# A two-layer graph attention kernel: where the first norm's steps, the softmax reciprocals and the adjacency mask are made

## The reference

```python
h = relu(layernorm(x)); q, k, v = heads(h@Wq+bq), heads(h@Wk+bk), heads(h@Wv+bv)   # 16 heads of 32
scores = where(adj == 0, -inf, q @ k.T / sqrt(32))
x = x + (softmax(scores, -1) @ v) @ Wo + bo
h = relu(layernorm(x))
alpha = maximum((h@wq) @ (h@wk).T, 0) * (adj != 0)
alpha = softmax(alpha, axis=1)                       # over the rows
x = x + alpha @ (h @ weight)
```

## Time and profile before

| | |
|---|---|
| median of 3 runs | 1620.14 us (1619.84 to 1623.53) |
| profiled execution | 1615.62 us |
| its span, first to last instruction | 1613.8 us |
| TensorE (PE) busy | 1498.3 us, 93% |
| VectorE busy | 1316.8 us, 82% |
| ScalarE busy | 1129.5 us, 70% |
| GpSimd busy | 1018.6 us, 63% |
| granted TensorE clock, mean | 0.996 of full |
| HBM read and written | 57.94 and 16.78 MB, 46 GB/s |

### The profile page before, as it was taken

How to read it: one execution, slowest core, us unless ns; L and a number is a source line. 1 busy time by engine, 2 the same in 40 slices (tenths; PEclk the granted TensorE clock), 3 DMA queues, 4 the chain that set the end, 5 groups by cost and what they waited for, 6 DMA issues and landing times.

```text
span 1613.8 us, 50717 instructions
## 1 busy us (share of the span) xinstructions
PE 1498.3 (93%) x16561; PEld 1102.2 (68%) x16561; DVE 1316.8 (82%) x4202; ACT 1129.5 (70%) x2477; POOL 1018.6 (63%) x1286
## 2 busy tenths in 40 slices
PE   2889999999999999999999999999999999999996
PEld 1556777776777767677777677776667777767763
DVE  6788888888888888888888888888888888888773
ACT  3657776777777777777777777777777777777761
POOL 1556667667666766666766766676666676666561
PEclk9999999999999999999999999999999999999998
DMA  8758767666667765766766666676676676676660
GB/s 234 134 105 143 140 129 156 149 141 145 137 130 149 156 148 128 151 139 129 157 149 140 146 137 129 151 156 145 129 151 137 130 158 149 139 147 137 122 123 33
DMA packets 656197, 226.27 MB, mean 140 GB/s; under 512 B 611488, under 2 KB 627872, under 8 KB 656160
## 3 DMA queue, kind: packets, MB, share of 16 engines
q1 hardware_dynamic: 636848, 188.57, 58.1%
q10 hardware_dynamic: 19312, 37.23, 7.9%
HBM read 57.94 MB, written 16.78 MB: 46 GB/s over the span
## 4 chain that ended last, share of the span: by engine, by line
PE 53%; DVE 27%; issue 11%; ACT 4%; POOL 1%; DMA 1%; DVEq 1%; ACTq 0%; POOLq 0%; SPq 0%
PE ring L409 43%; DVE wk_raw L865 9%; PE pv L484 3%; PE score L465 3%; DVE heads_t_lo L959 2%; PE ring L519 2%; DVE newton L908 2%; DVE stage L946 2%; DVE o_sum L880 2%; DVE work L985 1%; DVE l_max L1000 1%; PE pv L486 1%; ACT val L668 1%; DVE e_lo L1016 1%; POOL wv_raw L1124 1%
## 5 line engine op out<-in xcount | busy, mean ns | idle before, releaser
L1124 POOL TENSOR_TENSOR wv_raw<-wk_raw,wv_raw 128x512 f16<-128x512 f32 x512 | 594.2, 1163 | 428.7 <-ACT wv_raw L639 428.5
L626 ACT ACTIVATE wk_raw<-wk_raw,least 128x256 f32<-128x256 f32 x1024 | 458.9, 497 | 8.4 <-DVE least L865 8.3
L865 DVE CUSTOM_DVE_ANT_0 wk_raw<-score,far,undo_score 128x256 f32<-128x256 f32 x1024 | 443.8, 477 | 11.7 <-DVE far L1036 11.4
L639 ACT ACTIVATE wv_raw<-wk_raw 128x512 f16<-128x512 f32 x512 | 320.4, 626 | 9.5 <-issue 4.5
L484 PE MATMUL pv<-val,turned 128*128 128x65 f16 x2048 | 185.8, 192 | 25.5 <-DVE o_sum L880 21.3
L484 PEld LDWEIGHTS pv<-val,turned 128*128 128x128 f16 x2048 | 148.3, 97 | 88.7 <-issue 39.6
L1143 POOL TENSOR_TENSOR heads_out<-o_sum,o_rcp 128x64 f32<-128x64 f32 x512 | 154.4, 323 | 76.2 <-DVE o_sum L880 72.7
L409 PE MATMUL ring<-wv_hi,h 128*128 128x256 f16 x1024 | 188.8, 273 | 1.6 <-DVE wv_lo L828 1.6
L409 PE MATMUL ring<-h,wq_hi 128*128 128x256 f16 x1024 | 175.5, 273 | 7.6 <-DVE wk_lo L828 7.6
L486 PE MATMUL pv<-val,turned 128*128 128x33 f16 x2048 | 177.9, 179 | 0.0
L409 PE MATMUL ring<-h,wk_hi 128*128 128x256 f16 x1024 | 175.1, 273 | 0.0
(11 more groups left out here) (147 smaller groups left out, 3570.9 us busy)
## 6 DMA issues: line engine op xcount, KB each, us to landing
xin<-x_dram ACTq DMA_DIRECT2D x32, 512.0 KB, 3.7
out_dram<-xo SPq DMA_DIRECT2D x32, 512.0 KB, 3.6
xa<-x_dram ACTq DMA_DIRECT2D x31, 512.0 KB, 4.1
adj_in<-adj_dram SPq DMA_DIRECT2D x32, 256.0 KB, 2.8
turned<-wv_raw SPq DMA_TRANSPOSE x512, 3.1
adjt_in<-adj_t_dram SPq DMA_DIRECT2D x32, 256.0 KB, 3.2
wq_raw<-wq_dram SPq DMA_DIRECT2D x2, 512.0 KB, 6.0
wk_raw<-wk_dram SPq DMA_DIRECT2D x2, 512.0 KB, 7.6
```

Source lines behind the costliest of these rows:

```text
L626: last = nc.scalar.activation(probs[:, at, q, :], probs[:, at, q, :], ACT.Exp, bias=least[:, at, q:q + 1], scale=-1.0)
L639: nc.scalar.activation(halves[:, at, :, 0, :], probs[:, at, :, :], ACT.Copy).then_inc(hi["p"], 1)
L865: last = nc.vector.tensor_tensor_reduce(out=probs[:, at, q, :], in0=score[u % GROUP][:, q * NODES:(q + 1) * NODES], in1=far[:, q, :], scal ...
L1124: nc.gpsimd.tensor_tensor(halves[:, at, :, 1, :], probs[:, at, :, :], halves[:, at, :, 0, :], ALU.subtract).then_inc(lo["p"], 1)
```

## The change

Four things:

- `far` is written by GpSimd itself, in step 11 in place of step 8, after the last mask of the present graph has been made (`masked`). `far_next` and VectorE's copy are gone; VectorE's first mask of the next graph waits for GpSimd (`far_ok`), and so does SyncE's load of the next `adj_in`.
- The Newton step of the first norm is taken by GpSimd at the head of `first_normalise`, as six instructions on two columns, the last four of which wait for the one before. Both are in step 12 now (`NORM1`), behind the writing of `far` in GpSimd's order. VectorE's `reciprocal_deviation` is left for the second norm only.
- `second_reciprocal` is put ahead of the mask in VectorE's step 12.
- The low part of the second half of the nodes is made in step 2 behind that step's dense tiles, not in step 1 ahead of them.

```diff
-STATS1, ROOT1, NORM1, LATE_MASK = (8, 9), 10, 11, 5
+STATS1, ROOT1, NORM1, LATE_MASK = (8, 9), 10, 12, 5
-HIGH1_STEP, LOW1_STEPS, TURN1_STEP = 14, (0, 1), 6
+HIGH1_STEP, LOW1_STEPS, TURN1_STEP = 14, (0, 2), 6
-X1_STEP, XIN_STEP, KEEP_STEP, FAR_STEP = 1, 4, 4, 8
+X1_STEP, XIN_STEP, KEEP_STEP, FAR_STEP = 1, 4, 4, 11
...
                     if s == ADJ_STEP and nxt:
                         if started(t):
-                            sp.wait_ge(far_next_ok, count(t, 1, 0))
+                            sp.wait_ge(far_ok, count(t, 1, 0))
...
@@ VectorE, body @@
-                    if s == HEADS - MASKS_AHEAD[0][0] and nxt:
-                        dve.wait_ge(far_next_ok, count(n, 1, 0))
-                        if cur:
-                            dve.wait_ge(masked, count(t, HEADS, HEADS - 1))
-                        nc.vector.tensor_copy(far[:], far_next[:]).then_inc(far_ok, 1)
+                    if s == AL_STEP + 1 and prev:
+                        second_reciprocal(p)
                     for by in MASKS_AHEAD[s % GROUP][:1 if s == LATE_MASK else 2]:
...
-                        reciprocal_deviation(1, p)
+                        reciprocal_deviation(p)
                         second_normalise(p)
-                    if s == NORM1 and later:
-                        reciprocal_deviation(0, n + 1)
                     if s == AL_STEP + 1 and prev:
-                        second_reciprocal(p)
                         second_low(p)
                     if s in STATS1 and later:
                         first_stats(STATS1.index(s), n + 1)
-                    if s in LOW1_STEPS and cur and nxt:
-                        first_low(LOW1_STEPS.index(s), n)
+                    if s == LOW1_STEPS[0] and cur and nxt:
+                        first_low(0, n)
                     for name in DENSE[s]:
...
+                    if s == LOW1_STEPS[1] and cur and nxt:
+                        first_low(1, n)
                     if s == LATE_MASK and cur:
...
@@ GpSimd @@
             def first_normalise(b):
-                pool.wait_ge(negated, count(b, 1, 0))
+                y, a, c = rstd[0][:], newton[0][:, 1, :], newton[0][:, 2, :]
+
+                def step(ins, at):
+                    ins.then_inc(nstep[0], 1)
+                    pool.wait_ge(nstep[0], count(b, 2 * NSTEPS, at))
+                    settle(pool, pool_settled)
+
+                pool.wait_ge(rooted[0], count(b, 1, 0))
                 settle(pool, pool_settled)
+                nc.gpsimd.tensor_scalar(minus_mean[:], meanvar[0][:, :, 0], -1.0, None, ALU.mult
+                                        ).then_inc(nstep[0], 1)
+                nc.gpsimd.tensor_scalar(c, meanvar[0][:, :, 1], EPS, -1.0, ALU.add, ALU.mult
+                                        ).then_inc(nstep[0], 1)
+                step(nc.gpsimd.tensor_tensor(a, y, y, ALU.mult), 2)
+                step(nc.gpsimd.tensor_tensor(c, a, c, ALU.mult), 3)
+                step(nc.gpsimd.tensor_scalar(c, c, 1.5 / ROOT, None, ALU.add), 4)
+                step(nc.gpsimd.tensor_tensor(y, c, y, ALU.mult), 5)
                 for q in range(QT):
...
-                    if s == NORM1 and later:
-                        first_normalise(n + 1)
                     if s == X1_STEP and prev and not started(p - 1):
...
                     if s == (FAR_STEP if cur else 0) and nxt:
                         pool.wait_ge(adj_got, count(n, 16, 15))
                         if started(t):
-                            pool.wait_ge(far_ok, count(t, 1, 0))
+                            pool.wait_ge(masked, count(t, HEADS, HEADS - 1))
                         settle(pool, pool_settled)
                         for q in range(QT):
-                            last = nc.gpsimd.tensor_scalar(far_next[:, q, :], adj_in[:, q, :], 0,
+                            last = nc.gpsimd.tensor_scalar(far[:, q, :], adj_in[:, q, :], 0,
                                                            FAR, ALU.is_equal, ALU.mult)
-                        last.then_inc(far_next_ok, 1)
+                        last.then_inc(far_ok, 1)
+                    if s == NORM1 and later:
+                        first_normalise(n + 1)
```

More of the change, by code:

```diff
@@ L263, in two_layers @@
         far_ok = sem("far_ok")
-        const_ok, negated = sem("const_ok"), sem("negated")
+        const_ok = sem("const_ok")
         logged = [sem("logged1"), sem("logged2")]
@@ L272, in two_layers @@
             sem("dve_settled"), sem("pool_settled"), sem("sp_settled"))
-        x1_ok, keep_ok, far_next_ok = sem("x1_ok"), sem("keep_ok"), sem("far_next_ok")
+        x1_ok, keep_ok = sem("x1_ok"), sem("keep_ok")
         RELEASE = {"v1": (lo["v"], 2, 1), "v0": (lo["v"], 2, 0),
@@ L897, in first_stats, with reciprocal_deviation @@
                     aggregate(0, b)
-            def reciprocal_deviation(which, b):
-                y, a, c = rstd[which][:], newton[which][:, 1, :], newton[which][:, 2, :]
+            def reciprocal_deviation(b):
+                y, a, c = rstd[1][:], newton[1][:, 1, :], newton[1][:, 2, :]
                 def step(ins, at):
-                    ins.then_inc(nstep[which], 1)
-                    dve.wait_ge(nstep[which], count(b, NSTEPS, at))
-                dve.wait_ge(rooted[which], count(b, 1, 0))
+                    ins.then_inc(nstep[1], 1)
+                    dve.wait_ge(nstep[1], count(b, NSTEPS, at))
+                dve.wait_ge(rooted[1], count(b, 1, 0))
                 step(nc.vector.scalar_tensor_tensor(out=a, in0=y, scalar=-1.0, in1=y,
                                                     op0=ALU.mult, op1=ALU.mult), 0)
-                step(nc.vector.scalar_tensor_tensor(out=c, in0=meanvar[which][:, :, 1], scalar=EPS,
+                step(nc.vector.scalar_tensor_tensor(out=c, in0=meanvar[1][:, :, 1], scalar=EPS,
                                                     in1=a, op0=ALU.add, op1=ALU.mult), 1)
@@ L913, in reciprocal_deviation @@
                                                     op0=ALU.add, op1=ALU.mult), 2)
-                if which == 0:
-                    nc.vector.tensor_scalar(minus_mean[:], meanvar[0][:, :, 0], -1.0, None,
-                                            ALU.mult).then_inc(negated, 1)
             def second_normalise(b):
@@ L1084, in _ @@
                 first_stats(q, 0)
-            reciprocal_deviation(0, 0)
             for q in range(QT):
```

1 line of the change is left out of this document (removed).

## The result

| | before | after |
|---|---|---|
| median | 1620.68 us (1619.84 to 1623.53) | 1571.09 us (1567.43 to 1573.56) |
| profiled execution | 1615.62 us | 1570.80 us |
| its span | 1613.8 us | 1569.0 us |
| TensorE busy | 93% | 96% |
| VectorE busy | 1316.8 us | 1247.9 us |

The ratio is 0.9694, 95% interval 0.9679 to 0.9708. Both medians are of four executions. The prediction was 1580 us with a range of 1568 to 1618. In the profiled executions the gain is 44.8 us of span; the median moved by 49.6, since the profiled execution before was 5.1 us under its median and the one after only 0.3 under.

A forecast was written before the change was run, and what follows sets the result against it. The prediction took TensorE, nearly full, to be bound by two waits a graph for VectorE. 0.67 + 1.07 - 0.31 - 0.13 = 1.30 us a graph, 31 times, less 1 us at the start, gave 1580 us, range 1568 to 1618.

The forecast's parts named there:

- A: TensorE's head product at 718.55 waits 0.58 us for VectorE's sums (`o_sum`); forecast to go, counted as 0.67 a graph.
- B: Second half of wo0 on TensorE at 728.50 waits 1.07 us for VectorE's `heads_t_lo`; forecast to go entirely.
- 0.31 us given back: At layer 2's start: without low halves g0 came 12.44 us after wo0's second half, against 12.13; 0.31 a graph lost.
- another 0.13: Moved low half between wo0's statistics and wo1's residual: some 0.54 us later, 0.41 of it slack, 0.13 a graph lost.
- C: First matmul of g0 on TensorE at 740.63, 12.13 us behind wo0's second half; forecast some 12.6 behind it.
- I count 0.2 us: VectorE's step 11 without the Newton step: the two-column scaling ends at 710.2 instead of 710.4, a gain of 0.2 us.
- inside this, not on top: Step 12: time won on the copy of `far` counted within the 0.9 us by which the sums come earlier.
- Nothing charged: GpSimd's step 12: head 15's subtraction some 0.5 us later, with time until 717.4, so no cost.
- Rival 1: Moved low half meets GpSimd's subtraction, stands 1.16 us; g0 1.2 later, 0.1 us a graph left, 1617 us; chance 0.25.
- Rival 2: Step 12: `xa` on GpSimd delays `e_lo` up to 1.0 us; gain 0.7 us a graph, 1599 us; chance 0.13.
- Rival 3: GpSimd's six small instructions in step 12 take 5.9 us, deciding from 4.8: 1.1 a graph slower, 1654 us; chance 0.09.
- Rival 4: TensorE's stalls are not what the listed releasers say, so nothing moves: 1620 us; chance 0.03.

The follow-up runs named there:

- e1_low_moved: Kernel before with only the second low half moved to the end of step 2: 1588.89 us, ratio 0.9812, 46.59 us a graph.
- e2_low_back: Changed kernel with the second low half back in step 1 ahead of `heads_t_lo`: 1594.62 us, ratio 0.9849, 46.91 us a graph.
- e8_newton_alone: Kernel before with only the first norm's Newton step and normalise moved to GpSimd's step 12: 1603.24 us, ratio 0.9897, 47.15 us a graph.
- e3: Changed kernel with `second_reciprocal` back behind the mask of step 12: 1568.52 us, ratio 0.9689, 45.85 us a graph.
- e6: Kernel before with the low half moved and `second_reciprocal` ahead of the mask, nothing else: 1569.05 us, ratio 0.9696, 45.85 us a graph.
- e7: Changed kernel with `far_next` written by GpSimd in step 8 and VectorE's copy in step 12 back: 1569.18 us, ratio 0.9684, 45.85 us a graph.
- e10_newton_8: Changed kernel with eight more small Newton instructions on GpSimd in step 12, same value: 1650.08 us, ratio 1.0197, commonest graph 48.2 us.
- e11_newton_4: Changed kernel with four more small Newton instructions on GpSimd in step 12, same value: 1594.73 us, ratio 0.9869, commonest graph 46.7 us.
- e5: Kernel before with only `second_reciprocal` moved ahead of the mask, behind the copy of `far`: 1597.09 us, ratio 0.9858, 46.91 us a graph.
- e4_newton_back: Changed kernel with the Newton step back on VectorE in step 11, GpSimd's normalise kept in step 12: 1591.53 us, ratio 0.9830.
- e12_half_behind: Changed kernel with an unused maximum on VectorE ahead of the moved low half: 1600.66 us, ratio 0.9901, 46.95 us a graph.

## Why the prediction was right, and where not

**Stalls A and B as the whole of what bounds.** Right. B was put at 1.07 us and was worth 1.07 (e1_low_moved) and 1.06 (e2_low_back). A was put at 0.67 and was worth 0.75: the idle time of 0.58 is reckoned from a modelled matmul end, and my addition of 0.09 for that was half of what it should have been. From the first matmul ahead of A to A's, by starts, it is 2.04 us before and 1.30 after, 0.74 less.

**"0.31 us given back" and "another 0.13".** This is the step that failed. It took 0.44 us a graph off a gain that was not reduced there, 12 us over 27 graphs. I took C's distance of 12.44 us from the last graph, which has no low halves, as the floor. It was not one: that graph had a wait of its own, 0.20 us for a transpose, and ran at other offsets. The changed kernel kept 12.15, which is TensorE's own work, since it is busy nearly throughout the graph. But the place is as tight as I feared in another sense: with 0.48 us of filler a graph grew by 0.48. Both hold together if the slack there is just used up, and a row of the changed kernel's list of waits (350 to 1400 us) says so: ahead of the transposes of the second norm TensorE's weight load (PEld) waits 0.3 us for the qk3 pair in every graph, its matmuls don't. The kernel before has no such entry. The wait in the last graph before, and this row:

```profile
1545.87 0.20 PE L484 MATMUL pv<-val,turned 128*128 128x65 f16 x1 [0.20 <-DMA turned<-wv_raw]
```

```profile
PEld ring L518 <- DVE stage L942: 5.9, 23, 0.3
```

**The sum.** 0.67 + 1.07 - 0.44 was 1.30 us a graph; measured were 1.81 in an undisturbed graph and 1.73 as a mean over 27, since TensorE now loses time at one head product in some graphs. That is 11.6 us more than forecast for these 27. The forecast had four more graphs at 1.30, less 1 us at the start, which is 4; there 2 us were given back, 6 less than forecast. So the span moved by 44.8 where 39 were forecast: two errors of which one hid half of the other. The other 5 us between 49.6 and 44.8 are the distance of the profiled executions from their medians, and no merit or fault of the working. The 1571 of the median is inside the range, 3 us from its end.

**Newton step, "I count 0.2 us".** Mis-sized: alone it is worth 0.51 us a graph. That the next item "waits for TensorE's `al`" was true only in part: in e8_newton_alone the maximum's first instruction (`work`) started 29.85 us behind the residual add where it had started at 30.21, 0.36 earlier. The rest is the scaling behind it, 0.23 long where it had been 0.40. In the change it was not held by the writing of `far` either, as I had assumed.

**Copy and reciprocals.** That A would go with time to spare was right. The working charged the parts to one another correctly ("inside this, not on top"), but did not say that two of them are not needed; e3, e6 and e7 show it.

**Small instructions of GpSimd.** 1.8 us forecast, 2.43 measured: 0.19 to 0.24 each instead of 0.17, and one held by `e_lo`. "Nothing charged" was right. What was not is how much it has in hand. My limit of 717.4 for the subtraction of head 15, against its start near 715.6, puts the begin of the cost at some 3.5 us for the six; by the two runs it is about 3.2, 0.8 above what they take. I had looked at the transpose of head 15 and left out the mask that waits for its subtraction.

**Rivals.** Rival 1 was a matter of 0.1 us, as said, and VectorE was first. That it was first is luck as much as reckoning: the prediction gave it twice the chance of the other. Its price of 1.2 us a graph is for a half that meets the whole subtraction; the run that brought the collision about measured 0.8 for it. Rival 2 did not occur, since `e_lo` came ahead of `xa`, at 740.84 against 742.40. Whether `xa` in front would have held it no run shows. In e8_newton_alone `e_lo` was in front by 0.1 us, at 708.72, and there it was `xa` that stood, 2.00 us for its two in place of 1.53:

```profile
708.83 2.00 POOL L1140 TENSOR_SCALAR xa<-xa,minus_mean,rstd 128x512 f32<-128x512 f32 x2 [0.22 <-POOL rstd L1138]
```

Rival 3 has the right mechanism, and a price that is too low. Its 4.8 us is not where the cost begins but where it eats up the 1.3 us won; by its own working 3.94 us cost some 0.4 a graph and 5.43 some 1.9, and 0.8 and 2.4 were measured. The expectations of e10_newton_8 and e11_newton_4 read the 4.8 as the begin. e10_newton_8 is 2% slower than before. Rival 4 is out, by e1 and e5.

## What to carry to other kernels

When an in-order engine feeds the bounding one, list the stalls of the bounding engine in one period and treat each as a width: edits ahead of it in the same queue add up only until it is closed, so that the cheapest one per stall is enough (here two moved calls, e6_low_recip, gave all of what four parts gave). Then test each part by taking it back and by making it alone, since the two answers differ. When the bounding engine is busy for the whole period (here 45.83 of 45.85 us), stop: what is left is its own work. And where VectorE and GpSimd both read SBUF, a small shift can change who is first: here 0.3 us of shift made a graph 1.1 us longer, 0.8 of it by the collision.

## What the runs showed of the hardware that was not expected

Two-column instructions of VectorE were held by GpSimd's TENSOR_TENSOR for as long as that had left: 0.94 at 696.15 and 0.97 at 699.34 in e4_newton_back. The float32 TENSOR_SCALAR that makes `xa` held one too: in e6_low_recip the scaling took 0.40 at 738.89, and `xa`'s two ended at 739.26 (737.74 plus 1.52). The TENSOR_SCALARs that write `far` and `keep` from integers hardly did. In e4_newton_back VectorE's two-input instructions at 697.13 and 697.50 took 0.33 and 0.16 inside a write of `far` that ran until 699.17; in e6_low_recip, with GpSimd idle beside them, both took 0.16. In the changed kernel all 22 first instructions of the second norm's Newton step between 350 and 1400 us took 0.15 to 0.16 us; the one at 716.29 ran inside GpSimd's `keep`:

```profile
716.29 0.16 DVE L907 SCALAR_TENSOR_TENSOR newton<-rstd 128x2 f32<-128x2 f32 x1
```

```profile
715.97 2.38 POOL L1181 TENSOR_SCALAR keep<-adjt_in 128x256 bf16<-128x256 int32 x2
```

GpSimd did not pay for it: the first of the two, beside which the Newton step ran, took 1.08 us, as `far`'s do (1.07). The second took 1.32, and beside it ran VectorE's normalise of the second norm (1.08 us for two, from 716.88); no run settles why. The page "SBUF — State Buffer" of the Trainium skill (Who interferes with whom) has a VectorE instruction with two SBUF inputs contend with any GpSimd instruction that reads SBUF, the later one blocked until the end of the other. The rows agree for GpSimd's two-input instructions (1.47 against 0.67 in e12_half_behind) and for `xa` (2.00 against 1.53 in e8_newton_alone). They do not for `far` and `keep`, and the measurement decides.

A memset of VectorE, which reads nothing, held GpSimd's two-input subtraction: with it and the half the pair took 3.38 us, with the half alone 2.89, and 2.28 undisturbed. The second of the pair took 2.09 of the 3.38, so it is recorded from 718.25 on, 0.06 ahead of the memset's 718.31, and was held all the same. Recorded starts this close do not say who is first; the durations do.
